# Two runs of unread products before the first maxima, both low parts on VectorE, and Pool's last pads behind the first maxima

## What is computed

```python
q = (hidden @ Wq.T).reshape(B, S, H, D)      # H = 32 heads, D = 8, S = 1024
k = (hidden @ Wk.T).reshape(B, S, H, D)
v = (hidden @ Wv.T).reshape(B, S, H, D)
q, k = _apply_rope(q, cos, sin), _apply_rope(k, cos, sin)
scores = einsum('bhid,bhjd->bhij', q, k) * scale + bias    # bias on a band of 128, causal
m = maximum(max(scores, axis=-1), off)
p = exp(scores - m[..., None])
denom = sum(p, axis=-1) + exp(off - m)
out = einsum('bhij,bhjd->bhid', p, v) / denom[..., None]
x = x + out @ Wo.T
```

## Time and profile before

| | |
|---|---|
| median of 3 runs | 1070.26 us (1066.79 to 1070.7) |
| the profiled execution | 1068.44 us |
| its span | 1066.5 us |
| mean granted TensorE clock | 0.973 |
| PE busy | 970.4 us (91%) |
| DVE busy | 744.2 us (70%) |
| ACT busy | 572.4 us (54%) |
| POOL busy | 398.6 us (37%) |

### The profile page before, as it was taken

The page is one execution under the profiler, slowest core; times in us unless marked ns, Lnnn a source line. Parts: engine busy times, 40 slices in busy tenths (PEclk is TensorE's granted clock), DMA queues, the critical chain, the costliest instruction groups (busy, mean ns, idle before and its releaser), DMA issues.

```text
span 1066.5 us, 20863 instructions
## 1 busy us (share of the span) xinstructions
PE 970.4 (91%) x7835; PEld 664.8 (62%) x7860; DVE 744.2 (70%) x1865; ACT 572.4 (54%) x1167; POOL 398.6 (37%) x261
## 2 busy tenths in 40 slices
PE   4999779999999999999988879999999999999697
PEld 2687613333443343588767657777777777777586
DVE  7756965989888884454676767777767677777644
ACT  5543413666766667644464555555655555565263
POOL 3010230045234531000144056565655656566154
PEclk9999957999999999999999999999999999999898
DMA  4020542355424502022010000000000000000001
GB/s 109 1 83 1 153 95 37 60 101 91 75 68 90 96 22 72 1 80 80 1 40 1 0 2 1 2 2 1 2 2 2 2 1 2 1 2 2 1 1 40
DMA packets 25372, 37.92 MB, mean 36 GB/s; under 512 B 3096, under 2 KB 21192, under 8 KB 23752
## 3 DMA queue, kind: packets, MB, share of 16 engines
q1 hardware_dynamic: 25272, 36.59, 14.5%
HBM read 30.53 MB, written 5.85 MB: 34 GB/s over the span
## 4 chain that ended last, share of the span: by engine, by line
PE 32%; DVE 8%; issue 5%; ACT 4%; POOL 2%; ACTq 0%; DVEq 0%
PE bank L1108 14%; PE pair L1533 7%; PE bank L1574 4%; PE bank L1562 3%; DVE mx L1947 3%; PE bank L1209 3%; POOL P L827 2%; ACT QH L835 1%; ACT P L1030 1%; DVE xn L1674 1%; PE bank L1138 1%; DVE CT L1989 1%; DVE stats L1664 1%; DVE hL L1731 0%; DVE WQ L1916 0%
## 5 line engine op out<-in xcount | busy, mean ns | idle before, releaser
L827 POOL TENSOR_SCALAR P<-P,rec 128x1024 f32<-128x1024 f32 (+7 forms) x128 | 220.1, 1724 | 175.7 <-DVE rec L1972 175.7
L956 ACT ACTIVATE PT<-bank 128x512 f32<-128x512 f32 (+2 forms) x320 | 154.4, 559 | 110.7 <-PE bank L1345 92.5
L1810 DVE CUSTOM_DVE_ANT_0 bank<-bank,stripS 128x128 f32<-128x128 f32 (+1 forms) x224 | 129.9, 605 | 28.1 <-PE bank L1272 27.0
L1533 PE MATMUL pair<-KH,QH 128*128 128x512 f16 (+3 forms) x576 | 115.0, 327 | 16.4 <-ACT P L1030 13.6
L1030 ACT ACTIVATE P<-pair,nm 128x1024 f32<-128x1024 f32 (+7 forms) x128 | 95.5, 746 | 56.1 <-DVE nm L1951 56.0
L1574 PE MATMUL bank<-PT,VH 128*128 128x128 f16 x1728 | 117.2, 219 | 0.1
L1272 PE MATMUL bank<-KT,QT 96*128 96x512 bf16 (+2 forms) x336 | 103.0, 331 | 10.3 <-DVE MX L1810 8.4
L1574 PEld LDWEIGHTS bank<-PT,VH 128*128 128x128 f16 x1728 | 107.0, 98 | 2.9 <-DVE PT L1980 0.2
L1980 DVE TENSOR_TENSOR PT<-bank,PT 128x384 f16<-128x384 f32 (+1 forms) x192 | 99.8, 548 | 11.6 <-ACT PT L835 11.6
L1725 DVE TENSOR_TENSOR hf<-sil,bank 128x512 f32<-128x512 f32 x64 | 44.0, 687 | 86.4 <-PE bank L1108 57.8
L1947 DVE TENSOR_REDUCE mx<-pair 128x1 f32<-128x1024 f32 (+7 forms) x128 | 95.8, 749 | 10.7 <-PE pair L1535 10.7
(11 more groups left out here) (186 smaller groups left out, 1937.6 us busy)
## 6 DMA issues: line engine op xcount, KB each, us to landing
KT<-qk_dram SPq DMA_DIRECT2D x21, 192.0 KB
stripS<-band_rows SPq DMA_DIRECT2D x28, 128.0 KB, 2.2
qk_dram<-parts SPq DMA_DIRECT2D x12, 256.0 KB, 2.1
stripT<-seq_dram SPq DMA_DIRECT2D x27, 88.0 KB, 8.5
q_raw<-w_gu SPq DMA_DIRECT2D x4, 512.0 KB, 10.3
w_raw<-w_dense SPq DMA_DIRECT2D x2, 1024.0 KB, 6.6
w_raw<-w_q SPq DMA_DIRECT2D x2, 1024.0 KB, 5.3
QT<-qk_dram SPq DMA_DIRECT2D x14, 128.0 KB
```

The costliest lines, as they stand in the source:

```text
L827: pool.tensor_scalar(rows, rows, rec1[:, m % 4:m % 4 + 1], None, ALU.mult).then_inc(s["pn"], 1)
L956: act.activation(PT[:, n % 4, hs[0]:hs[-1] + 1, 0:ni], src, ACT.Exp).then_inc(s["s2_exp"], 1)
L1533: ins = pe.matmul(out, QH1[:, h % 2, l, P * ib:P * (ib + 1)], KH1[:, r, h // (H1 // GR), HALF * c:HALF * c + nj], start=(i == 0), stop=(i ...
L1810: dve.tensor_tensor_reduce(out, out, stripS[:, h, HALF - nj:HALF], 1.0, LOWEST, ALU.add, ALU.max, mx).then_inc(s["s1_max"], 1)
```

## The change

Four edits. VectorE makes the low part of unit 2 too, ahead of that of unit 3; SP's waits for the two low parts of the second half follow. Pool loses that low part, and its pads of group 1 wait for all four low parts. Pool's pads of group 2 wait for the six operations of the first maxima. TensorE gets 8 products of `keep_clock` ahead of pair 3, behind a wait for the last eviction of the values (they use bank 6), and 12 behind pair 7, ahead of the transposes of the first maxima.

```diff
@@ sync
-                for u, done, n in (((0, "p_lo_d", 1), (1, "p_lo_d", 2)), ((2, "p_lo", 1), (3, "p_lo_d", 3)))[half]:
+                for u, done, n in (((0, "p_lo_d", 1), (1, "p_lo_d", 2)), ((2, "p_lo_d", 3), (3, "p_lo_d", 4)))[half]:
                     sp.wait_ge(s[done], n)
                     write_part(u, 2)
@@ gpsimd
-            pool.wait_ge(s["p_mid"], 3)
-            pool.tensor_tensor(parts[:, 2, 2, :, :], rt[:, 2, :, :], parts[:, 2, 1, :, :], ALU.subtract).then_inc(s["p_lo"], 1)
             pool.wait_ge(s["v_mm"], TB // 2)
-            pool.wait_ge(s["p_lo"], 1)
+            pool.wait_ge(s["pool_cst"], 12)
+            pool.wait_ge(s["p_lo_d"], 4)
             pad_rows(1)
...
                 if g == 0:
                     pool.wait_ge(s["vst"], 1)
+                    pool.wait_ge(s["m_ops"], M_OPS)
                     pad_rows(2)
@@ tensor, look1_pair
                 elif 3 <= n < 8:
+                    if n == 3:
+                        pe.wait_ge(s["v9"], TB // 2)
+                        keep_clock(bank[6], 8)
                     pe.wait_ge(s["s1_max"], 2 * (n - 2))
@@ tensor, attention
                 for n in range(8):
                     look1_pair(n)
+                keep_clock(bank[6], 12)
                 maxima(0, 0)
@@ vector, qkv
                 rest(2)
                 rest(3)
+                low(2)
                 low(3)
                 dve.wait_ge(s["pool_cst"], 12)
```

## The result

The changed kernel takes 1062.93 us in the median of 20 executions, the kernel before 1067.97 in as many: 5.0 us less. The ratio is 0.995, 95% interval 0.9934 to 0.9965. I had forecast 11.9 us less, 1058.4, with a range of 1055 to 1067. The time lies where rival B had put it. One execution of a later experiment ("The later fills only") took 1124.52 us at a mean clock of 0.845; it is left out of that run's ratio but not of its median, which would be 1061.53 without it.

The account below looks back on a forecast made before the run. TensorE at half clock from about 134.2 to 171.8 us was taken as the limit. 2.2 us ahead of the transposes plus 9.7 behind them made 11.9, so 1070.26 became 1058.4 us, range 1055 to 1067.

Parts of the forecast that it names:

- rival B: Among pairs 8 to 13 the clock falls again because TensorE is sparse: 1062 to 1066.5 us, middle 1065; chance 0.33.
- from the transposes to the second maxima: The chain of pairs 8 to 23 at full clock takes 20.5 us instead of 30.2, 9.7 us less.
- the held clock: Case A: full clock held throughout, all 11.9 us gained, 1058.4 us; chance 0.45.
- the bound of 159: Between transposes and second maxima VectorE alone has 15.1 us of reductions, so the second maxima come at 159 at best.
- A's own range: Range of the case with full clock throughout: 1055.5 to 1061 us, from second maxima at 159 and 165.
- Ahead of the transposes: Transposes of the first maxima start at 141.9 instead of 144.10, 2.2 us earlier.
- The low parts: Both on VectorE at 1.22 us each, ahead of the first reduction, which starts 0.8 us earlier.
- The pads: Pool's pads of group 2 move behind the first maxima, so the first CAST is not slowed: 0.74 us saved.
- The twelve products: Behind pair 7 they end at 141.9, mostly covered by VectorE's work to 141.6, and cost 0.3 us.
- Rival C: Fills do not hold the clock, run at half clock and delay the transposes 3.1 us: 1073.4 us; chance 0.07.
- Rival D: Second half's loads, the maxima's DMA or the second look cause waits instead; 3 to 4 us lost, 1062; chance 0.12.

Follow-up runs that it names:

- The later fills only: Changed kernel without its own two fills, but with 4, 4 and 3 unread products ahead of pairs 10, 12 and 14: 1061.86 us, ratio 0.9934.
- the kernel with two later fills: Changed kernel plus 4 and 4 unread products ahead of pairs 10 and 12, none ahead of pair 14: 1058.13 us, ratio 0.9896.
- three more fills: Changed kernel plus 4, 4 and 3 unread products ahead of pairs 10, 12 and 14: 1058.01 us, ratio 0.9904.
- two kernels with five fills: The kernel with three more fills, 1058.01 us, and that kernel with the low part of unit 2 back on Pool, 1058.85 us.
- the kernel without the first fill: The kernel with three more fills, without the 8 products ahead of pair 3: 1058.0 us, ratio 0.9899.

## Why the prediction was right and wrong

*The bound was read rightly.* The stretch at half clock was what the fills could win, and where the clock is held the gain is close to the sum: 10.9 us in the trace of the kernel with two later fills and 11.5 in its medians (1069.66 to 1058.13), for 11.9 forecast.

*The step that failed is the one that joins the two halves of the sum,* the full clock "from the transposes to the second maxima". I took 9.7 us for it; the changed kernel's trace gives 30.23 - 27.75 = 2.48. The working had the warning in it: TensorE busy 0.93 of each link of 2.3 us. So had the rows: even at half clock pairs 10 and 12 stood behind waits of 1.08 and 0.87 us, and I filled neither. Rival B named the place (a fall between 144 and 149; it was 145.0) and the time (1062 to 1066.5; it was 1062.93), and I gave it 0.33 against 0.45 for the held clock. Of the 20 executions of the changed kernel four lie between 1056.5 and 1058.2, with a mean clock of 0.988 to 0.990, eleven between 1061.9 and 1064.1 at 0.980 to 0.984, and five above 1065 at 0.974 to 0.977. So my likeliest case is what one in five does, as far as times and mean clocks can tell; only one execution was traced. The five slowest come close to the clock of the kernel before (0.969 to 0.976 in the executions beside the experiments), so in them the change seems to have won next to no clock; none of them was traced. The row from 612 to 618, at full clock with half of it idle, speaks for a held clock (my text has it as "for it" under B, which reads the other way); it was one stretch of other work and proved nothing for this one.

*B's mechanism and its price fit.* I had priced a single fall at 3.8 us of gain and up to 8 where the clock returns early; the trace's 4.4 and the 5.0 of the medians lie between.

*Some of the nearness of the time is luck.* I subtracted from 1070.26, the median of three executions; twenty gave 1067.97. From there my sum would have said 1056.1. Of the 11.9 us that I forecast the change brought 5.0, so the gain is 6.9 off and the time only 4.5. (A slip beside it: from the bound of 159 A's own range starts at 1055.0, not 1055.5.)

*Ahead of the transposes the sum was right, what its terms are worth was not.* 2.2 us forecast, 1.95 measured from the landmark. The low parts, forecast 0.8: they do take 2.43 instead of 3.2 with its wait, and the first reduction starts 0.8 earlier, but VectorE then idles 0.98 us for pair 3, which stands behind the fill, so they are worth nothing beside the fill; the kernel with neither fill shows the 0.8. The pads, forecast 0.74: as a difference between the two traces that is right (the CAST 0.83 and 0.18), but taken out beside the fills the edit costs 2.0 to 2.2 at the transposes (15.4 to 15.7 from the landmark, for 13.4), because the full clock moves the CAST into the whole of the memsets. I took its price from a trace in which the CAST met only the end of them. The twelve products, forecast 0.3: measured 0.4.

*The skill's rule held.* By the Trainium skill, GPSIMD Engine Reference, section 8 (Key points), GpSimd contends with VectorE instructions with two SBUF inputs or in a mode that uses both ports. Here the low parts at 1.22 against 2.04 us agree, and the reductions out of PSUM are not slowed (1.22 to 1.23 for 1024 columns, beside a memset and without). The CAST, 0.18 against 2.72, has one input, and no trace tells in which mode it ran. What it costs I could only have read off the length of the memsets, had I asked where the CAST goes once TensorE is faster.

The Trainium skill, TensorE: Matmul & The Clock Gate, Part 1, says that the point at which the clock changes varies from run to run of the same kernel. The stretch ahead of the change, where the instructions are the same in all kernels, agrees: behind a wait of TensorE of 3.51 to 3.52 us that ends at about 115 to 117 us, the clock was low from 117.2 for 3.4 us in the profiled execution before, from 114.3 for 6.8 us in the changed kernel's, and did not fall at all in that with three more fills.

*Rival C* as a whole happened in the kernel with the second fill alone; its first part, a first fill at half clock, in the profiled executions of two kernels with five fills (3.78 and 3.65 us for the 8 products instead of 2.11), where the twelve products then ran at full clock again. *Rival D* did not: in the changed kernel and the one with two later fills no DMA released pair 8 or the first tile of the second look.

*What stays open:* why one execution holds the clock where the next does not. The trace shows only one execution of each kernel, and they differ already ahead of the change. The length of a wait does not settle it: the clock fell behind waits of 2.34 and of 1.18 us and held through one of 3.51. Nor do the runs tell whether the fills work by filling the waits or by the kind of their products, which have 128 rows and fp32r operands where the pairs have 96 and bf16; fills of the pairs' own kind would. And whether the low part on Pool costs 0.8 us in executions whose first fill is slow.

## What to carry to other kernels

A fill of unread products is worth what the clock is worth until the next sparse place, so look for all of them at once, with the durations of the full clock: where TensorE waits for another engine at half clock it is sparser still at full clock, and there the clock can be lost again. (Pairs 8 to 13 were busy 7.30 of the 10 us from 144 to 154 before, and 2.52 of 4 where the changed kernel lost it.) Price each edit once more in the schedule that the others make: one term vanished (the low parts behind the fill), another nearly tripled (the pads beside the CAST). And where a kernel's executions lie 6 us apart, read the trace from a landmark ahead of the change, and count how many executions do what the profiled one does.

## What the hardware showed that I had not expected

Once the clock was down, work that looked nearly seamless did not bring it back for long: in the kernel before, TensorE was busy 15.83 of the 16 us from 154 to 170, mostly with bf16 products of 96 and of 128 rows, and the clock stayed at 0.50 until 171.8. It came back during runs of 12 products of 128 rows and 512 columns in fp32r: 2.6 us into the run in the kernel without the first fill (the 12 took 4.20 us), and 4.1 us into it in the one with the second fill only. And a small CAST of 128x16 took 2.72 us instead of 0.18, and ended when Pool's second memset of 1.80 us did.
